# A two-head graph attention kernel: the last four chunks of a pass by column halves, a hand-ordered last group, and ELU in two VectorE operations

## The reference, cut to what matters

```
x = _layernorm(x + gcn(x, adj))
x_norm = _ln(x, g1, b1);  mask = (adj > 0) | eye
for i in range(K):
    h = x_norm @ ff0_w[i].T
    e = leaky_relu(s_src[:, None] + s_dst[None, :])     # s_src, s_dst = h @ attn_w[i] halves
    atten = softmax(where(mask, e, NEG), axis=1)
    att = _ln(atten @ h + x, g2, b2)
    h_next = h_next + elu(att @ ff1_w[i].T) / K
x = _layernorm(x + h_next)
```

## Time and profile before

| | us |
|---|---|
| Median of 3 runs | 1063.94 (1062.9 to 1065.08) |
| The profiled execution's own time | 1063.9 |
| Its span, first to last instruction | 1062.1 |
| TensorE busy | 986.0 (93%) |
| VectorE busy | 701.0 (66%) |
| ScalarE busy | 499.0 (47%) |
| GpSimd busy | 113.6 (11%) |

### The profile page before, as it was taken

How to read it: one execution, slowest core, us unless ns; L and a number is a source line. 1 busy time by engine, 2 the same in 40 slices (tenths; PEclk the granted TensorE clock), 3 DMA queues, 4 the chain that set the end, 5 groups by cost and what they waited for, 6 DMA issues and landing times.

```text
span 1062.1 us, 9255 instructions
## 1 busy us (share of the span) xinstructions
PE 986.0 (93%) x2590; PEld 477.6 (45%) x2592; DVE 701.0 (66%) x1251; ACT 499.0 (47%) x723; POOL 113.6 (11%) x144
## 2 busy tenths in 40 slices
PE   5789999999999999999769999999999999999980
PEld 4334444444644444444655444444545444444440
DVE  0567766654355444344737767888799998988874
ACT  3433332221200000001266765978686888888754
POOL 0011111111040000000800000000010101010111
PEclk8899999999999999999769999999999999999995
DMA  9999999999286999995023131222222232323201
GB/s 347 427 426 427 428 426 425 425 422 388 110 322 256 371 377 383 385 380 213 1 70 99 62 97 59 91 79 97 72 70 86 84 99 89 99 90 100 84 5 40
DMA packets 62202, 226.03 MB, mean 213 GB/s; under 512 B 4496, under 2 KB 44112, under 8 KB 52048
## 3 DMA queue, kind: packets, MB, share of 16 engines
q1 hardware_dynamic: 57040, 208.56, 51.3%
q10 hardware_dynamic: 5120, 17.01, 4.0%
HBM read 205.59 MB, written 19.96 MB: 212 GB/s over the span
## 4 chain that ended last, share of the span: by engine, by line
PE 77%; DMA 11%; ACT 5%; POOL 3%; issue 2%; DVE 2%; SPq 1%; POOLq 0%; ACTq 0%; DVEq 0%
PE ps L1096 77%; DMA W<-in_adj 11%; ACT W L478 2%; POOL rstd L419 1%; POOL r L426 1%; ACT T L558 1%; ACT final L604 1%; SPq L302 0%; DVE T L870 0%; ACT mix L587 0%; ACT squares L578 0%; POOL rs L437 0%; POOL r L424 0%; POOL r L425 0%; POOLq L82 0%
## 5 line engine op out<-in xcount | busy, mean ns | idle before, releaser
L1096 PE MATMUL ps<-colbuf,stat 128*128 128x512 f32 x992 | 441.9, 602 | 25.3 <-DVE diag L712 24.8
L1096 PE MATMUL ps<-T,Yw 128*128 128x512 f32 x1024 | 445.1, 594 | 9.2 <-DVE T L870 9.2
L870 DVE SCALAR_TENSOR_TENSOR T<-T,mring 128x2048 f32<-128x2048 f32 x128 | 292.5, 2287 | 66.6 <-ACT T L558 65.9
L558 ACT ACTIVATE T<-Rrow,small,ratio 128x1024 f32<-128x1024 f32 x256 | 301.3, 1230 | 70.7 <-PE ps L1096 70.4
L1096 PEld LDWEIGHTS ps<-T,Yw 128*128 128x128 f32 x1024 | 195.4, 191 | 245.4 <-issue 230.7
L1096 PEld LDWEIGHTS ps<-colbuf,stat 128*128 128x128 f32 x992 | 187.9, 193 | 248.9 <-issue 220.8
L478 ACT ACTIVATE W<-W 128x4096 f32<-128x4096 f32 (+30 forms) x32 | 66.1, 2067 | 147.7 <-DMA W<-in_adj 147.7
L497 ACT ACTIVATE stat<-xw_g 128x128 f32 (+1 forms) x32 | 9.9, 310 | 197.8 <-PE ps L1096 167.8
L751 DVE TENSOR_SCALAR mtile<-colbuf 128x4096 uint8<-128x4096 f32 x30 | 69.7, 2323 | 11.6 <-DMA mask<-mtile 9.7
L747 DVE TENSOR_TENSOR colbuf<-colbuf,ident 128x128 f32 (+1 forms) x26 | 7.6, 291 | 88.3 <-DMA colbuf<-in_adjT 88.3
L672 DVE TENSOR_TENSOR W<-W,colbuf 128x3712 f32<-128x3712 f32 (+28 forms) x29 | 62.3, 2148 | 0.0
(11 more groups left out here) (150 smaller groups left out, 581.5 us busy)
## 6 DMA issues: line engine op xcount, KB each, us to landing
colbuf<-in_adjT SPq DMA_DIRECT2D x58, 2048.0 KB, 13.2
mring<-mask SPq DMA_DIRECT2D x128, 256.0 KB, 2.7
mask<-mtile ACTq DMA_DIRECT2D x32, 512.0 KB, 10.2
Rrow<-s_src SPq DMA_DIRECT2D x9, 512.0 KB, 4.1
W<-in_adj SPq DMA_DIRECT2D x2, 2048.0 KB, 14.7
W<-in_adjT SPq DMA_DIRECT2D x2, 2048.0 KB, 12.7
out<-final SPq DMA_DIRECT2D x6, 512.0 KB, 3.9
W<-in_xT SPq DMA_DIRECT2D x8, 256.0 KB, 6.9
```

The source lines that it names most:

```text
L558: last = act.activation(T[:, c % TS, j, :], Rrow[:, g % 2, :], ACT.Relu, scale=ratio[:, c * JB + j:c * JB + j + 1], bias=small[:, 8:9])
L870: v.scalar_tensor_tensor(out=tile, in0=tile, scalar=1.0, in1=mring[:, c % TS, :, :].rearrange("p b n -> p (b n)"), op0=ALU.add, op1=ALU.mu ...
L1096: return pe.matmul(*args, skip_group_check=True, **kw)
```

## The change

**Column halves.** In a pass's last group, chunks 12 to 15 first multiply the first column half only (`chunk_half` with part 0) and then all four the second half, in a new function `halves`. Only the second half counts `chunk_done`. The first half of the sums is copied (`copy_half`, 512 columns) as soon as its last matmul is done, and its fold runs after the second half of chunk 12. The second half's copy comes at s = 4 and its fold at s = 6 of the next group as before. `num_copied` now counts halves.

**Last group.** The end of the program is written out for each engine in an order of its own. The last group's second fold goes to banks 0 to 3. VectorE takes over `scale_y` and `add_bias` in one operation a block (`tail_y`) and `final_rows` (`tail_write`); the final layernorm runs by half groups (`tail_norm`, and two small GpSimd operations a half); the squares start block by block; the store is two DMAs of 256 KB, one a half.

**ELU.** The bias carries a further -1/K and the exponential a shift (scale K, bias 1 - ln K), so that the ELU and the residual are two operations: at s = 14 and 18 `max(y, -1/K) + residual`, and at s = 16 and 20 `min(exp, 1/K) + total`.

The diff, cut (imports, new tiles and semaphores and small renamings are left out):

```
 sp:
             store(last_phase - 3, G - 2)
-            store(last_phase - 2, G - 1)
+            for part in range(2):
+                sp.wait_ge(tail_ready, part + 1)
+                sp.dma_start(out_v[:, blocks_of(G - 1, part), :], tail_rows[:, half_of(part), :]).then_inc(stored, 16)
 pool:
+            row_scale(last_phase, 0)
             final_scale(last_phase - 3)
+            row_scale(last_phase, 1)
             for part in range(2):
-                row_scale(last_phase, part)
-            final_scale(last_phase - 2)
+                own = tail_scale[:, half_of(part)]
+                pool.wait_ge(tail_moments, part + 1)
+                pool.tensor_scalar(own, tail_mv[:, half_of(part), 1], LN_EPS, 1.0, ALU.add, ALU.mult).then_inc(tail_step, 1)
+                pool.wait_ge(tail_step, part + 1)
+                pool.tensor_tensor(own, own, half[:, 0:BPG], ALU.pow).then_inc(tail_scaled, 1)
 act:
+            def copy_half(q, part):
+                m = q * G + (G - 1)
+                if part == 0:
+                    act.wait_ge(half_done, at_turn(q + 1))
+                    act.wait_ge(fold_done, at_turn(m * 2))
+                else:
+                    act.wait_ge(chunk_done, at_turn(m * NC + (NC + TS)))
+                    act.sem_inc(act_gate, 1)
+                act.activation(numS[:, cols(part, GW)], ps[:, (G - 1) % 2 * 2 + part, :], ACT.Copy).then_inc(num_copied, 1)
-                if s == 4:
+                if s == 4 and k == G - 1:
+                    copy_half(last_pass, 1)
+                elif s == 4:
                     copy_sums(m, k)
...
+                copy_half(q, 0)
             last_phase = Count(more, 2 * G, 2 * G - 1)
...
+            scale_y(previous, 1, 1)
+            exp_y(previous, 1, 1)
+            tail_square(0)
+            copy_half(Count(more, 2, 1), 1)
+            final_rows(previous - 2, G - 2, ACC - 3, 0)
+            exp_y(last_phase, 1, 0)
+            tail_square(1)
+            final_rows(previous - 2, G - 2, ACC - 3, 1)
+            exp_y(last_phase, 1, 1)
 v:
+                total = plane(ACC - 3 * h, blocks)
                 if stage == 0:
+                    v.wait_ge(y_ready, at_turn(u + 1))
+                    v.scalar_tensor_tensor(out=total, in0=mixed_half(part, 1 - h), scalar=-1.0 / K,
+                                           in1=plane(X1 + 2 * h, blocks), op0=ALU.max, op1=ALU.add).then_inc(part_summed, 1)
+                else:
                     v.wait_ge(exp_y_ready, at_turn(u + 1))
-                    v.tensor_scalar(e, e, 1.0, 1.0 / K, ALU.min, ALU.mult).then_inc(elu_low, 1)
-                    v.scalar_tensor_tensor(out=e, in0=e, scalar=-1.0 / K, in1=mixed_half(part, 1 - h),
-                                           op0=ALU.add, op1=ALU.max).then_inc(elu_ready, 1)
-                    v.tensor_tensor(plane(ACC - 3 * h, blocks), plane(X1 + 2 * h, blocks), e, ALU.add).then_inc(sum_ready, 1)
+                    v.scalar_tensor_tensor(out=total, in0=mixed_half(part, h), scalar=1.0 / K,
+                                           in1=total, op0=ALU.min, op1=ALU.add).then_inc(sum_ready, 1)
...
+            elu(previous, 1, G - 2, 0, 1)
+            add_bias(previous, 1, 1)
+            for stage in range(2):
+                elu(previous, 1, G - 2, 1, stage)
+            take_sums(last_phase, G - 1, 0, False)
+            tail_mix(0)
+            for part in range(2):
+                final_stats(previous, 1, G - 2, part)
+            final_moments(previous - 2)
+            tail_y(0)
+            final_shift(previous - 2)
+            take_sums(last_phase, G - 1, 1, False, TAIL_BANK)
+            tail_mix(1)
+            for stage in range(2):
+                elu(last_phase, 1, G - 1, 0, stage)
+            tail_norm(0)
+            tail_y(1)
+            elu(last_phase, 1, G - 1, 1, 0)
+            tail_write(0)
+            elu(last_phase, 1, G - 1, 1, 1)
+            tail_norm(1)
+            tail_write(1)
 pe:
+            def chunk_half(q, g, c, part):
+                if part == 0:
+                    pe.wait_ge(t_made, at_turn(q * (G * NC) + (g * NC + c + TS + 1)))
+                for j in range(JB):
+                    last = multiply(ps[:, (g % 2) * 2 + part, :], Yw[:, c * JB + j, :], T[:, c % TS, j, cols(part, GW)],
+                                    start=False, stop=c == NC - 1 and j == JB - 1)
+                if part == 1:
+                    last.then_inc(chunk_done, 1)
+                elif c == NC - 1:
+                    last.then_inc(half_done, 1)
+            def halves(q, h):
+                for c in range(SPLIT, NC):
+                    chunk_half(q, G - 1, c, 1)
+                    if c == SPLIT:
+                        fold_sums(q * G + (G - 1), h, 0)
```

More of the change, by code:

```diff
@@ L645, in _, with tail_square @@
                             h = (turn >= more) if g >= back else (turn > more)
-                            ending(c + PHASE * (back - 1), q * G + (g - back), h, (g - back) % G, True)
+                            ending(c + PHASE * (back - 1), q * G + (g - back), h, (g - back) % G, True, q - 1)
+                copy_half(q, 0)
             last_phase = Count(more, 2 * G, 2 * G - 1)
[L648 to L651, removed]
+            previous = last_phase - 1
+            def tail_square(part):
+                for i in range(part * BPG, (part + 1) * BPG):
+                    act.wait_ge(tail_mixed, i + 1)
+                    last = act.activation(squares[:, i, :], mix[:, i, 0, :], ACT.Square, accum_out=sumsq[:, i:i + 1])
+                last.then_inc(squared, 1)
+            scale_y(previous, 1, 1)
[7 more added lines that the diff above has]
+            exp_y(last_phase, 1, 1)
         @block.vector
@@ L1001, in ending @@
                     add_bias(m, h, (s - 13) // 4)
[L1002 to L1004 removed]
+                if s in (14, 18):
+                    elu(m, h, k, (s - 14) // 4, 0)
+                if s in (16, 20):
+                    elu(m, h, k, (s - 16) // 4, 1)
                 if finish:
@@ new lines, in tail_y, with tail_norm @@
+            def tail_y(part):
+                v.wait_ge(rs_ready, at_turn(last_phase * 2 + part + 1))
+                v.sem_inc(dve_gate, 1)
+                for i in range(part * BPG, (part + 1) * BPG):
+                    last = v.scalar_tensor_tensor(out=mix[:, i, 0, :], in0=mix[:, i, 1, :], scalar=rs[:, i:i + 1],
+                                                  in1=y_bias[:, 1, :], op0=ALU.mult, op1=ALU.add)
+                last.then_inc(y_ready, 1)
+            def tail_norm(part):
+                v.wait_ge(sum_ready, at_turn(last_phase * 2 + part + 1))
+                v.sem_inc(dve_gate, 1)
+                for i in range(part * BPG, (part + 1) * BPG):
+                    last = v.bn_stats(tail_bn[:, i, :], W[:, Z0, (G - 1) * GB + i, :])
+                last.then_inc(tail_stats, 1)
+                v.wait_ge(tail_stats, part + 1)
+                for i in range(part * BPG, (part + 1) * BPG):
+                    last = v.bn_aggr(tail_mv[:, i, :], tail_bn[:, i, :])
+                last.then_inc(tail_moments, 1)
@@ L1283, in _ @@
                     for c in range(NC):
-                        chunk(q, g, c)
-                        ending(c, q * G + (g - 1), (turn >= more) if g >= 1 else (turn > more))
+                        if g == G - 1 and c >= SPLIT:
+                            chunk_half(q, g, c, 0)
+                        else:
+                            chunk(q, g, c)
+                        ending(c, q * G + (g - 1), (turn >= more) if g >= 1 else (turn > more), g >= 1)
+                halves(q, turn >= more)
             last_phase = Count(more, 2 * G, 2 * G - 1)
-            for s in range(PHASE):
-                ending(s, last_phase, 1)
+            pe.wait_ge(num_copied, at_turn(last_phase * 2 + 2))
+            for ib in range(BPG):
+                last = multiply(ps[:, TAIL_BANK + ib, 0:2 * C + 1], numS[:, cols(BPG + ib)], mixed[:, 1, :], start=True, stop=True)
+            last.then_inc(fold_done, 1)
 _INS = ["x", "xT", "adj", "adjT", "W1", "b1", "b2", "weights"]
```

83 lines of the change are left out of this document (54 added, 29 removed).

## The result

| | before | after |
|---|---|---|
| Median, us | 1064.71 (1062.9 to 1065.46, 5 runs) | 1058.53 (1057.54 to 1059.03, 5 runs) |
| Ratio | | 0.9941, 95% interval 0.993 to 0.9952 |
| Span of the profiled execution | 1062.1 | 1057.2 (its own time 1058.95) |
| TensorE, VectorE busy | 986.0, 701.0 | 988.1, 698.4 |

What follows compares the result with a forecast made beforehand. TensorE bounds the stream, an engine-to-engine chain the stretch after the last chunk. End gain 9.6 us less stream losses 0.8 + 2.1 = 2.9 gives 6.7, so 1063.9 becomes 1057.2 us; range 1054.3 to 1060.2.

Steps and rivals of the forecast that it cites:

- T(15) wanted three half chunks after chunk 12: Last group of each pass: TensorE halts for tile T(15), 0.8 us in pass 0 and 1.2 in the last pass.
- The ring late by 4.5 us: Start of pass 1: slots of the four-tile ring come free late, so VectorE's first mask starts 4.5 us late.
- The second halt: Pass 1's first group, before chunk 13: TensorE waits 2.1 us for a tile from late VectorE; bounds 0 and 3.5.
- from chunk 3 on: Pass 1's start: TensorE begins 2.5 us later but meets one fold fewer, so from chunk 3 only 0.8 later.
- the border: Passage from pass 0 to pass 1: halts of 0.8 and 2.1 us, 2.9 lost ahead of the last group.
- The end: From the last group's column halves to the program's end: span ends at 1052.5 instead of 1062.1, gaining 9.6 us.
- the wait at `final_shift`: After the stream: VectorE waits some 1.1 us at `final_shift` for GpSimd's power.
- the last store: Program's end: 2.7 us from the last store's issue to the end, against 3.5 before; bounds 2.3 and 3.5.
- The ring refills: Rival, pass 1's first group: no halt at chunk 13, VectorE's work moving into the border wait; 1055.1 us, chance 0.18.
- GpSimd held by VectorE: Rival, the end: VectorE's work slows four GpSimd pairs by 0.5 to 0.7 us each, 2.4; 1059.6 us, chance 0.12.
- The clock falls at a halt: Rival, behind TensorE's 2.1 us halt: the clock drops, price 1.7 us; 1058.9 us, chance 0.06.
- Slower: Rival, T(13) of pass 1's groups: ring never fills again, TensorE loses 14.8 us; 1069.1 us, chance 0.04.

Runs made afterwards that it cites:

- Kernel 2: Changed kernel with the split at chunk 13 instead of 12 and ScalarE's first half copy behind the next pass's first relus; 1055.83 us, ratio 0.9911.
- kernel 3: Changed kernel with VectorE reading the early fold (part 0 of a pass's last group) at step 3 instead of 7; 1059.66 us, ratio 0.9944.
- kernel 1: Changed kernel with the column halves starting at chunk 13 instead of 12, nothing else; 1059.65 us, ratio 0.9949.
- kernel 4: Changed kernel with only chunk 15 split, the half copy behind the next pass's third-chunk relus and, at the end, behind `scale_y`; 1058.32 us, ratio 0.9935.
- kernel 7: Changed kernel with the ELU in three operations again, at the steps used before the change; 1063.22 us, ratio 0.9986.

## Why the prediction was right, step by step

- *T(15) wanted three half chunks after chunk 12.* Forecast 0.8 and 1.2 us, idle time measured 0.70 and 0.97.
- *The ring late by 4.5 us.* Measured 4.8.
- *The second halt.* The mechanism, VectorE without a gap from the late mask on, is right, and so nearly is the size: 2.1 forecast, 2.2 measured (1.51, 0.27 and about 0.4). The place was wrong. The step that failed is "from chunk 3 on" to "a second halt at chunk 13": I followed the tiles only. The fold before chunk 7 waits for VectorE's reading of part 0, which before ended at 817.45 + 1.62 = 819.07, 1.2 us ahead of the fold at 820.31, and the next group's first fold for ScalarE's copy, which now ends at 868.04. The first of these waits took the halt that I had put at chunk 13. With small losses around the restarts the border cost 3.7, not 2.9. That the sum came within 0.5 us of the measured gain is in part luck: the border was 0.8 dearer than forecast and the end 0.4 better, and the two partly offset.
- *The end.* 9.6 forecast, 10.0 measured. `tail_y` 1.11 (taken as 1.1), the wait at `final_shift` 1.29 (1.1), the last store 2.5 us from its issue to the end (2.7). The exponential was dearer than its row, 0.72 instead of 0.63 us, with the bias read from a tile; it costs 0.09 us once, where VectorE waits for it (the ELU at 1031.58).
- *The ring refills* (rival): excluded by the trace. Kernel 2 shows what it would take.
- *GpSimd held by VectorE* (rival): hardly. After the stream its power took 1.39 once instead of 1.01, and one small operation 0.36 instead of 0.20, 0.5 us in all and not the 2.4 of the rival. In kernel 3 the rival did strike, inside the stream: 2.04 us instead of 0.20 beside a mask. The Trainium skill (GPSIMD Engine Reference, Specifications) names VectorE instructions in a 2-port mode or with two SBUF inputs as the ones that contend. The trace agrees for the 2.29 us masks, beside one of which the small operation takes 1.09 us (at 1024.85, while chunks stream); in the end such instructions are short, 0.69 at most, and so is what they add.
- *The clock falls at a halt* (rival): not in the changed kernel, whose folds behind 1.51 and 0.77 us take 2.00 us at clock 1.00; but in kernels 1, 4 and 7, behind 2.46, 4.90 and 2.45. The Trainium skill (TensorE: Matmul & The Clock Gate, HAM oscillation) states that waits between bursts of matmuls throttle the clock again; the traces agree in those three kernels, and not for the shorter halts.
- *Slower* (rival): no. By chunk 7 of the second group the folds and chunks run without a halt.

The 1.4 us by which the profiled execution of the changed kernel enters the passes later are scatter of the clock. The median difference doesn't contain them, and the experiments' traces lie between 0.5 us earlier and 1.2 us later than the kernel before at that place. Of the 1.4, 0.98 arise in the matmuls around 540 (`ps<-gff`): the granted clock is 1.00 from 541 on in the kernel before, but 0.50 there and 0.76 from 542 to 543 in the changed one. The other 0.40 are in the first eight chunk records behind a wait of 8.20 us, 5.66 instead of 5.26. In kernel 1, whose code up to there is the changed kernel's, the clock is 1.00 already from 540 to 541, so the change is not the cause. Why the clock rises at different moments stays open.

## What to carry to other kernels

When a buffer ring feeds the bound engine, freeing its slots late, or filling them late because a waiting instruction stands in front in the filling engine's queue, is a debt that the next busy stretch pays, at whatever wait comes first on any engine that hangs on the late one; list the PSUM and copy waits with the tiles, and ask how few slots can be held back for the same gain (three instead of four here, with the copy moved behind the next work, kept the 3 us at the end and gave 2.8 of the 3.7 at the border back; three without moving the copy gave nothing back). At a program's end order each in-order queue so that no instruction waits in front of one whose input is ready. An operation saved on an engine is worth its time where that engine is late: here 4.8 us beside the new order and at most 1.5 in the old one.

## What the runs showed that was not expected

Behind a halt of TensorE the next eight fold records took 2.00 us when the halt had been between 0.77 and 2.13 us long, with the granted clock at 1.00, and 3.45, 3.65 and 3.52 us behind halts of 2.46, 2.45 and 4.90 us (kernels 1, 7 and 4; mean clock 0.55, 0.57 and 0.59 in the 3 or 4 us around the fold). So the fold itself cost some 1.5 us more. What that costs the kernel depends on what waits for the fold: in kernel 4 nothing, because the fold ends at 1038.89 and VectorE, held at `final_shift`, reads the sums at 1039.15; in kernel 7 a part of it only, as said there. In kernel 1 it is the largest part of what made the split at chunk 13, without the moved copy, no better than the one at 12.
